# Weighted sums in sixteen short groups instead of eight long ones, two picking steps instead of four, and b1 added by VectorE's copy

## The reference

```
hi = x @ W1[:H];  hj = x @ W1[H:]
h  = relu(hi[:, :, None, :] + hj[:, None, :, :] + b1)      # 128 x 128 pairs of 128 numbers
y  = layernorm(h @ W2 + b2) * gamma + beta
out[b, i] = sum over j of adj[b, i, j] * y[b, i, j]
x  = layernorm(x + out)
```

## Time and profile before

| | |
|---|---|
| median of 3 runs | 2313.31 us (2313.24 to 2314.52) |
| the profiled execution, whole | 2314.34 us |
| its span in the trace | 2312.4 us |
| PE busy | 2283.6 us, 99% |
| ACT busy | 2220.4 us, 96% |
| VectorE busy | 2151.7 us, 93% |
| POOL busy | 2014.8 us, 87% |
| mean granted TensorE clock | 0.998 of full |

### The profile page before, as it was taken

The page is one execution under the profiler, slowest core; times in us unless marked ns, Lnnn a source line. Parts: engine busy times, 40 slices in busy tenths (PEclk is TensorE's granted clock), DMA queues, the critical chain, the costliest instruction groups (busy, mean ns, idle before and its releaser), DMA issues.

```text
span 2312.4 us, 168912 instructions
## 1 busy us (share of the span) xinstructions
PE 2283.6 (99%) x71240; PEld 2074.1 (90%) x71240; DVE 2151.7 (93%) x18204; ACT 2220.4 (96%) x3649; POOL 2014.8 (87%) x1227
## 2 busy tenths in 40 slices
PE   7999999999999999999999999999999999999997
PEld 7888899999999999999999999999999999999985
DVE  7999999999999999999999999999999999999997
ACT  7999999999999999999999999999999999999996
POOL 7988888988988888888888888898888888988884
PEclk9999999999999999999999999999999999999999
DMA  1000000000000000000000000000000000000000
GB/s 21 9 16 14 13 16 12 15 16 10 16 16 10 16 13 14 16 10 16 16 10 16 13 14 16 10 16 16 10 16 12 14 16 10 16 16 10 16 11 9
DMA packets 103861, 32.15 MB, mean 14 GB/s; under 512 B 77888, under 2 KB 103104, under 8 KB 103104
## 3 DMA queue, kind: packets, MB, share of 16 engines
q1 hardware_dynamic: 101808, 21.15, 4.4%
q10 hardware_dynamic: 1296, 0.20, 0.0%
HBM read 17.11 MB, written 4.19 MB: 9 GB/s over the span
## 4 chain that ended last, share of the span: by engine, by line
PE 97%; ACT 2%; DVE 1%; issue 0%; ACTq 0%; DMA 0%; DVEq 0%
PE y_ps L557 75%; PE agg_ps L596 20%; PE work_ps L557 2%; ACT h L280 1%; ACT y L275 1%; DMA beta_rows<-in_L_gnn_beta_dram 0%; DVE squares L543 0%; DVE vmean L413 0%; DVE o_sb L455 0%; DVE x_out L535 0%; DVE work_ps L473 0%; DVE work_ps L520 0%; DVE work_ps L469 0%; DVE st L524 0%; ACT ln L339 0%
## 5 line engine op out<-in xcount | busy, mean ns | idle before, releaser
L264 POOL TENSOR_TENSOR h<-abT 128x1024 f32<-128x1024 f32 x1024 | 1941.9, 1918 | 242.4 <-PE y_ps L557 231.7
L557 PEld LDWEIGHTS y_ps<-w_pair,h 128*32 128x32 f32 x65536 | 1916.8, 110 | 182.0 <-issue 142.5
L557 PE MATMUL y_ps<-w_pair,h 128*32 128x128 f32 x65536 | 1960.2, 273 | 4.5 <-DVE bias_rows L426 2.7
L543 DVE CUSTOM_DVE_ANT_0 squares<-y_ps,y 128x128 bf16<-128x128 f32 x8192 | 1843.7, 284 | 100.3 <-ACT y L275 85.2
L280 ACT ACTIVATE h<-h,b1c 128x1024 f32<-128x1024 f32 x1024 | 1192.1, 1164 | 9.2 <-POOL h L264 9.2
L275 ACT ACTIVATE y<-y_ps 128x508 f32<-128x508 f32 x2048 | 1136.0, 602 | 49.4 <-PE y_ps L557 43.7
L543 DVE DVE_READ_ACCUMULATOR2_ANT q<- 128x1 f32 x8192 | 678.1, 83 | 0.0
L596 PE MATMUL agg_ps<-y,wz 128*32 128x512 f32 x4096 | 588.1, 594 | 3.9 <-DVE work_ps L473 3.9
L596 PEld LDWEIGHTS agg_ps<-y,wz 128*32 128x32 f32 x4096 | 172.3, 110 | 9.6 <-issue 9.6
L238 POOL TENSOR_TENSOR wz<-adjT,rstd 128x128 f32<-128x128 f32 x64 | 34.8, 544 | 33.3 <-ACT rstd L313 33.3
L557 PEld LDWEIGHTS work_ps<-x1s,adjS 128*32 128x32 f32 x512 | 29.4, 110 | 31.7 <-issue 22.9
(11 more groups left out here) (89 smaller groups left out, 576.7 us busy)
## 6 DMA issues: line engine op xcount, KB each, us to landing
x_in<-in_x_dram SPq DMA_DIRECT2D x256, 16.0 KB, 1.9
adj_in<-in_adj_dram SPq DMA_DIRECT2D x256, 16.0 KB, 1.9
x_res<-in_x_dram SPq DMA_DIRECT2D x64, 64.0 KB, 2.0
adj_res<-in_adj_dram SPq DMA_DIRECT2D x64, 64.0 KB, 2.9
out_dram<-x_out SPq DMA_DIRECT2D x64, 64.0 KB, 1.7
w<-in_L_gnn_W_dram ACTq DMA_DIRECT2D x1, 64.0 KB, 2.1
ww<-in_L_gnn_W_w_dram ACTq DMA_DIRECT2D x1, 64.0 KB, 2.3
w1a<-in_L_gnn_W_dram SPq DMA_DIRECT2D x1, 64.0 KB, 2.5
```

Of the source, the lines that this page charges most:

```text
L264: nc.gpsimd.tensor_tensor(h[:, u % HRING].rearrange("k (r g) s -> k r g s", g=GROUPS), abT[:, p, 1, :].unsqueeze(1).unsqueeze(1).broadcast ...
L543: last = nc.vector.tensor_tensor_reduce(out=squares[:, (first_bank + k) % YRING, n, :], in0=y_ps[(first_bank + k) % YRING][:, n, :], in1=y ...
L557: last = nc.tensor.matmul(dst[cols], lhsT[:, cols], rhs, start=True, stop=True, tile_position=(0, g * GROUP))
```

## The change

CHUNK becomes 2. So `wz` has 16 chunks per group (its array grows from 1024 to 2048 numbers per partition, and so does the memset of L255), a weighted-sum group is four matmuls of 256 columns, and there are 16 of them. The new `SUM_AT` puts one behind each of the units 4, 5, 6, 8, 9, 11, 12 and 14 and two behind 7, 10, 13 and 15. The picking has two steps. `project` copies the first projection and adds b1 to the second in a second instruction, and the relu has no bias operand; the built program carries there the constant 0.0 instead of a pointer to `b1c`.

```
-    CHUNK = 4
+    CHUNK = 2
     CHUNKS = GROUP // CHUNK
-    SUM_AT = {u: c for c, u in enumerate((4, 6, 7, 9, 10, 12, 13, 15))}
+    SUM_AT = (4, 5, 6, 7, 7, 8, 9, 10, 10, 11, 12, 13, 13, 14, 15, 15)
...
-                nc.scalar.activation(h[:, u % HRING], h[:, u % HRING], ACT.Relu, bias=b1c[:, 0:1]).then_inc(h_ready, 1)
+                nc.scalar.activation(h[:, u % HRING], h[:, u % HRING], ACT.Relu).then_inc(h_ready, 1)
...
-                nc.vector.tensor_copy(abT[:, p, :, :], ab_ps).then_inc(ab_sb_s, 1)
+                nc.vector.tensor_copy(abT[:, p, 0, :], ab_ps[:, 0, :])
+                nc.vector.tensor_scalar(abT[:, p, 1, :], ab_ps[:, 1, :], b1c[:, 0:1], None, ALU.add).then_inc(ab_sb_s, 1)
...
-                    last = nc.tensor.matmul(agg_ps[g * GROUP:(g + 1) * GROUP, :], wz[:, g, chunk, :], y_chunk[:, :, g, :],
+                    last = nc.tensor.matmul(agg_ps[g * GROUP:(g + 1) * GROUP, 0:CHUNK * K], wz[:, g, chunk, :], y_chunk[:, :, g, :],
...
-                    if gather and u in SUM_AT:
-                        if SUM_AT[u] == 0:
+                    for chunk in (c for c in range(CHUNKS) if gather and SUM_AT[c] == u):
+                        if chunk == 0:
...
-                        weighted_sums(1 - p, SUM_AT[u])
+                        weighted_sums(1 - p, chunk)
```

## The result

| | before | changed |
|---|---|---|
| median of 6 runs, us | 2313.41 (2313.09 to 2314.79) | 2320.66 (2319.55 to 2328.84) |
| the profiled execution, whole, us | 2314.34 | 2323.22 |
| its span, us | 2312.4 | 2321.2 |

The ratio is 1.0036, 95% interval 1.0024 to 1.0048: slower by 7.3 us, above the forecast range (2310.5 to 2318.5). The prediction gave 12% to a time above 2317.9 us. The changed kernel also scatters more.

A forecast was written before the change was run, and what follows sets the result against it. PE's list of work was taken to bound the kernel from 62 to 2285 us. 2314.34 us profiled, +2.5 steady part, -0.9 start, -1.5 end, gave 2314.4, or 2313.4 us as a median; range 2310.5 to 2318.5.

The forecast's parts named there:

- PE in the steady part: Slots of the long stretch: 16 more passes in each of 64 slots at 2.4 ns each, +2.5 us.
- a short pass costs like two: Rival on the sums: a 256-column pass costs like two of 128 columns, +6.6 us in place of +2.5, 2317.5; 7%.
- Who might be late: Units 5 to 8 and chunk 0: PE meets no new wait, 0.39 us left at unit 5; nothing added.
- ACT and VectorE: Slots 2 to 63: each relu 80 ns cheaper, VectorE two picks fewer, all beside PE's work; zero gain.
- The start: Up to unit 4 of slot 1: ACT's chain starts 0.43 us later, 17 cheaper relus save 1.36; together -0.9 us.
- The end: From slot 64 on: fewer picking steps let PE's sums start 0.78 us sooner, and later picks save 0.78 again; -1.5 us.
- The clock at the end: Rival on the sums of slot 64: shorter PE idle time keeps the clock up, 1.7 us more gone, 2311.7; 10%.
- POOL's `wz`: Rival: POOL's product into `wz` gets slower and delays PE, 2339 at three times 544 ns; 9% with other waits.
- VectorE: Rival: VectorE was the hidden bound, so 64 slots save two steps of 0.37 us, 47 us, ending at 2266; 2%.
- weight loads: Rival: short groups are dear through their weight loads, 3.4 us more a slot, +218 us, 2531; 1%.

The follow-up runs named there:

- the third series: The changed kernel run once more, unaltered, in a later set of runs beside the kernel before: 2319.71 us, ratio 1.0034.

## Why the prediction was wrong

The step that failed is **"PE in the steady part"**. It took 1024 more passes at 2.4 ns each, +2.5 us, and said that a boundary costs nothing of its own. The size of that term is right: 61 periods x 0.04 = 2.4 us. What it left out is that each pass is eight instructions, and that their supply had almost no slack: one piece in 3.74 us at best, where a piece was used in 4.05 us before and is in 3.83 now. On average that still suffices. But through the five units without sums PE uses a piece in 3.49 us, quicker than one can come, so the time between the landing of a piece and its use shrinks. In the other eleven units it can grow again, and there a piece lasted (35.47 - 8.73) / (1604 / 256) = 4.27 us before and lasts 26.78 / (1732 / 256) = 3.96 us now. From the landing of a piece to the use of its first instruction the changed kernel has 2.0 us in the middle and 1.4 in the worst twentieth, the one before 2.5 and 1.6; at its 17 large gaps it has 1.2 to 1.6 us, and in no trace does PE begin a piece less than 1.15 us after the last landing. It fits that most of the excess lies in units 3 to 7 and 0. The stalls sum to 11.5 against 3.0 us: +8.5 us.

No single slow fetch makes a stall. Ten of the 17 gaps came after a fetch of under 1.2 us, and of the 71 pieces in slots 2 to 62 whose fetch took 1.35 us or more three began with such a gap. The pause from a landing to the next start varies too, from 2.4 to 3.2 us in nine tenths of the cases, and what counts is how the last few turns add up. The table shows, roughly, that executions with longer mean fetches have more stalls; the adding up is argued.

The statement that bore it was "the time is what PE's list of work takes". The q8 row stood on the page of before and I didn't hold it against PE's instruction count. Nor did any rival name it: "a short pass costs like two" (+6.6 us) would have come within 3.2 us of the time, by a mechanism that is not there.

The Trainium skill (TensorE: Matmul & The Clock Gate, Back-to-back issue gap) gives columns over the clock plus 2.5 ns for a matmul alone. By it, as an estimate, 1024 passes more cost 2.6 us, the +2.5 us of the forecast; the undisturbed periods here agree (+0.04 us for 16 passes), and the time of the kernel doesn't.

The other steps:

- **Who might be late.** Right: no wait of PE for `h`, `q` or L474 in the long stretch.
- **ACT and VectorE.** The relu lost 102 ns, not 80. It bought nothing in slots 2 to 63, as said. The 93 ns that the prediction takes from the Trainium skill (ScalarE: Activation LUTs) stand in its section What ACT_TABLE_LOAD costs, not in the one that is named there; they are nearer to the 102 ns of this trace than the 80 are.
- **The start.** The memset took 0.85 us more (forecast 0.9), the relu of unit 4 of slot 0 came 0.25 us later (0.43), that of slot 1 1.2 us sooner (0.9). From POOL and from ACT, the rows that answer to the earlier trace rows:

```profile
19.76 1.81 POOL L255 MEMSET wz<- 128x2048 f32 x1
```

```profile
23.48 1.06 ACT L280 ACTIVATE h<-h 128x1024 f32<-128x1024 f32 x1 [0.65 <-POOL h L264]
...
54.67 1.06 ACT L280 ACTIVATE h<-h 128x1024 f32<-128x1024 f32 x1
```

  In the profiled execution slot 2 begins 0.3 us earlier only, since PE stalls on instructions here too (0.5 us at 63.8). In the three other executions of this kernel it begins at 84.1 to 84.3 us, 1.0 to 1.2 before the 85.35 of the kernel before.
- **The end.** -1.8 us, forecast -1.5. PE's idle time before the sums of slot 64 went from 3.90 to 3.10 us and that in slot 65 from 6.30 to 5.45; these rows of PE answer to the earlier trace rows.

```profile
2301.42 5.61 PE L597 MATMUL agg_ps<-y,wz 128*32 128x256 f32 x72 [3.10 <-DVE work_ps L474]
...
2315.72 0.66 PE L558 MATMUL work_ps<-x1s,adjS 128*32 128x129 f32 x8 [5.45 <-ACT x1s L335]
```

- **The clock at the end.** Down, as forecast, in all but one of the profiled executions of the changed kernel (0.58 in the first, 0.64 in the third series); where it stayed at 1.00, the end was 1.9 us shorter, near the rival's 1.7. PE's idle time before it was the same, 3.12 us there and 3.10 here.
- **POOL's `wz`, VectorE, weight loads.** None: 536 ns; no gain for 27 us less of VectorE over the whole; a group has 0.43 us, so no rival on them came true.

The sum as measured: 2314.34 + 2.4 (passes) + 8.5 (stalls) - 0.3 (start) - 1.8 (end) = 2323.1, against 2323.22 us.

Open is what makes a fetch take 1.07 us on average in one execution and 1.10 to 1.15 in another, on the same chip too, what sets the pause before the next fetch, and whether the core's own transfers have a part in it where the fetches are long.

## What to carry to other kernels

When one engine is the bound, hold its number of instructions against the row of its instruction queue: packets, the time between them and the busiest stretch between two lighter ones. Splitting long matmuls in a stream of many short ones can cost more than their fixed part, and it shows as small waits on "issue", a multiple of 256 instructions apart, and as scatter from run to run. Where a finer division pays only at the ends, use it only there.

## What the runs showed of the hardware

- PE's instructions come in pieces of 256 (16.4 KB). In a stream of matmuls and weight loads that always waited for them one came each 3.74 us: 1.09 us for the fetch, 2.65 us to the next start. Column-tiled float32 products at 109 ns a pass use one in 3.49 us.
- Two 64-column tiles do a pass in the same 109 ns as four of 32 columns, with half the instructions; but each change between the widths costs 0.144 us.
- 7168 semaphore increments between products made the kernel 1149 us longer, 160 ns for each. Gaps at the first instruction of a piece summed to 995 us, and a piece came each 5.73 us.
- Reading the relu's bias from a column, not from a constant, costs 102 ns on 128x1024.
